# A graph-attention layer whose node tables come from one product of 288 columns, with every edge group gathered from the K/V table

## The reference

```
Q, K, V = x @ Wq + bq, x @ Wk + bk, x @ Wv + bv          # per node
E       = edge_attr @ We + be                            # per edge
score   = exp(clip(sum_d(K[src] * Q[dst] / sqrt(12) * E), -5, 5))   # per edge, head
h       = segment_sum(V[src] * score, dst) / (segment_sum(score, dst) + 1e-6)
out     = layernorm(x + h)
```

## Time and profile before

| what | value |
|---|---|
| timed runs | 1014.6 us median (1014.39 to 1017.43) |
| profiled execution, span | 1301.3 us (this span is all that is recorded of its own time) |
| mean granted TensorE clock in it | 0.729 |
| busy in the span | PE 672.6, PEld 461.0, DVE 653.2, ACT 177.1, POOL 748.1 us |
| DMA | 165.87 MB, 127 GB/s over the span |

### The profile page before, as it was taken

The page is one execution under the profiler, slowest core; times in us unless marked ns, Lnnn a source line. Parts: engine busy times, 40 slices in busy tenths (PEclk is TensorE's granted clock), DMA queues, the critical chain, the costliest instruction groups (busy, mean ns, idle before and its releaser), DMA issues.

```text
span 1301.3 us, 12054 instructions
## 1 busy us (share of the span) xinstructions
PE 672.6 (52%) x3352; PEld 461.0 (35%) x3352; DVE 653.2 (50%) x1307; ACT 177.1 (14%) x337; POOL 748.1 (57%) x788
## 2 busy tenths in 40 slices
PE   3834744755345464455564355545454565445343
PEld 3833422533223343333343233333333333333223
DVE  4311634864346554455554454555455555455446
ACT  1413101111011111011110111011011111111011
POOL 7172465265656665666666565666666666666640
PEclk8756866877677766767778676677767777677777
DMA  7643543544435444544545354544544445445420
GB/s 178 222 145 105 161 126 94 147 125 130 135 100 138 119 132 111 133 132 130 138 120 145 94 153 103 137 134 120 136 131 129 134 128 137 115 136 138 115 70 21
DMA packets 101206, 165.87 MB, mean 127 GB/s; under 512 B 45132, under 2 KB 63853, under 8 KB 101133
## 3 DMA queue, kind: packets, MB, share of 16 engines
q1 hardware_dynamic: 62829, 84.39, 23.4%
q0 software_dynamic: 37152, 75.74, 22.2%
q10 hardware_dynamic: 1152, 4.92, 0.9%
HBM read 152.57 MB, written 12.39 MB: 127 GB/s over the span
## 4 chain that ended last, share of the span: by engine, by line
another core or an unknown queue 40%; issue 22%; DVE 17%; PE 15%; ACT 4%; DMA 1%; DVEq 0%; SPq 0%
DVE qe L830 5%; PE psE L451 4%; DVE logit L919 4%; ACT qe L632 3%; PE psA L521 3%; PE psT L472 3%; DVE qke L910 2%; DVE clipped L925 1%; PE psQ L431 1%; DVE q_parts L809 1%; DVE ob L882 1%; PE psA L482 1%; DVE place L818 1%; DVE msg L937 1%
## 5 line engine op out<-in xcount | busy, mean ns | idle before, releaser
L390 POOL DMA_INDIRECT kv<-kv_table,idx x758 | 724.6, 956 | 514.3 <-issue 218.1
L521 PE MATMUL psA<-place,msg 128*104 128x104 f32 x1536 | 206.4, 301 | 339.7 <-DVE msg L937 253.5
L521 PEld LDWEIGHTS psA<-place,msg 128*104 128x104 f32 x1536 | 193.0, 212 | 369.9 <-DVE msg L937 270.5
L818 DVE TENSOR_TENSOR place<-psI,rel_tile 128x832 f32<-128x832 f32 (+1 forms) x99 | 98.6, 996 | 322.9 <-remote 322.9
L451 PE MATMUL psE<-ea,we 97*96 97x512 f32 x392 | 241.8, 750 | 0.8 <-ACT xt L613 0.8
L632 ACT ACTIVATE qe<-psE 96x1024 f32<-96x1024 f32 (+1 forms) x99 | 99.9, 1009 | 573.4 <-remote 432.5
L830 DVE TENSOR_TENSOR qe<-psQ,qe 96x1024 f32<-96x1024 f32 (+1 forms) x99 | 118.9, 1201 | 60.7 <-ACT qe L632 35.5
L472 PE MATMUL psT<-identity,qe 96*128 96x96 f32 x782 | 109.7, 297 | 74.5 <-DVE qe L830 56.2
L472 PEld LDWEIGHTS psT<-identity,qe 96*128 96x128 f32 x782 | 92.1, 174 | 88.9 <-DVE qe L830 63.8
L910 DVE TENSOR_TENSOR qke<-psT,kv 128x768 f32<-128x768 f32 (+1 forms) x99 | 92.9, 938 | 29.0 <-remote 25.1
L451 PEld LDWEIGHTS psE<-ea,we 97*96 97x96 f32 x392 | 71.5, 206 | 74.5 <-issue 73.5
(11 more groups left out here) (117 smaller groups left out, 405.6 us busy)
## 6 DMA issues: line engine op xcount, KB each, us to landing
ea<-eaT SPq DMA_DIRECT2D x99, 384.0 KB
q_parts<-rel_table SPq DMA_DIRECT2D x99, 252.0 KB
kv<-kv_table,idx POOLq DMA_INDIRECT x758
qwin<-q_table SPq DMA_DIRECT2D x198, 23.6 KB
xb<-xrows SPq DMA_DIRECT2D x24, 144.0 KB
out<-ob SPq DMA_DIRECT2D x24, 144.0 KB
q_table<-q_parts SPq DMA_DIRECT2D x4, 720.0 KB
kv_table<-kv ACTq DMA_DIRECT2D x2, 960.0 KB
```

Of the source, the lines that this page charges most:

```text
L390: pool.indirect_dma_start(kv[:, k, t], None, kv_table, sources).then_inc(kv_in[k], 16)
L521: last = nc.tensor.matmul(sums[0:ML, off:off + PW], msg[:, s, t], place[:, s, t], start=opens, stop=closes)
L818: nc.vector.tensor_tensor(place[:, k % 2, 0:nt], ps_ids.unsqueeze(1).broadcast_to([P, nt, PW]), rel_tile[:, bass.ds(g * T, nt)].unsqueeze( ...
```

## The change

- One product of 288 columns makes the K, V and Q rows of a tile. A pair fills two PSUM banks; three pairs of banks take turns. For each pair ACT makes two copies in place of one: K/V to `kv_stage`, and Q, scaled, to a new buffer `q_full`. PE waits for both copies of the pair three before.
- The ten Q blocks with their own products are gone. `leading` now reads `q_full` and runs between the pairs. `remainder` subtracts in place in `q_full`; five of the ten run before DVE waits for `ranges_all`, and five after the index tables. The middle and last parts follow as before.
- The special path of groups 0 to 2 is gone: raw gathers, transposes, `convert`. All 782 gathers are from `kv_table`, and the first waits for all of it and for the index load, which is now one transfer, issued once `range_up` is counted.
- `CLOSE` goes from 16 to 2: groups 2 to 15 are now also held until the query rows of group *at* - 2 are done.
- SP issues the node chunks with fewer waits, and stores `q_table` in eight chunks in place of six.

```
-CLOSE = 2 * U
+CLOSE = 2
-XG = 3
-Q_CHUNKS = (10, 10, 10, 10, 5, 5)
+EARLY_QUERIES = 5
+        q_full = sb("q_full", [P, NR // P, D], f32)
+        node_banks = [psE, psQ, psT]
@@ block.sync
-                        sp.dma_start(idx[:, 0:XG * T], src[:, 0:XG * T]).then_inc(idx_in, 16)
                         load_nodes(0)
+                        load_nodes(1)
                         sp.wait_ge(xt_in[0], 16)
-                        load_nodes(1)
...
-                        load_nodes(5)
+                        for c in range(5, len(KV_CHUNKS)):
+                            load_nodes(c)
                         sp.wait_ge(range_up, 1)
                         sp.dma_start(range_table..., ranges...).then_inc(range_out, 16)
-                        sp.wait_ge(xt_in[4], 16)
-                        load_nodes(6)
-                        load_nodes(7)
+                        sp.dma_start(idx[:], src).then_inc(idx_in, 16)
                         sp.wait_ge(range_out, 16)
...
-                        sp.dma_start(idx[:, XG * T:], src[:, XG * T:]).then_inc(idx_rest_in, 16)
...
-                            sp.wait_ge(q_up, (tile + size) // QB)
+                            sp.wait_ge(q_up, -(-(tile + size) // QB))
@@ block.gpsimd
                         if first and at == 0:
                             pool.wait_ge(idx_in, 16)
-                        if first and at == XG:
-                            pool.wait_ge(idx_rest_in, 16)
                             pool.wait_ge(kv_out, 16 * len(KV_CHUNKS))
...
-                            if first and at < XG:
-                                pool.indirect_dma_start(xg[:, k, t], None, xrows, sources).then_inc(xg_in[k], 16)
-                            else:
-                                pool.indirect_dma_start(kv[:, k, t], None, kv_table, sources
-                                                        ).then_inc(kv_in[k], 16)
+                            pool.indirect_dma_start(kv[:, k, t], None, kv_table, sources).then_inc(kv_in[k], 16)
@@ block.tensor
-                                if n >= 4:
-                                    pe.wait_ge(kv_up, n - 3)
+                                if n >= 3:
+                                    pe.wait_ge(kv_up, n - 2)
+                                    pe.wait_ge(q_full_up, n - 2)
                                 for j in range(2):
-                                    last = nc.tensor.matmul(kv_banks[n % 4][:, j * 2 * D:(j + 1) * 2 * D],
-                                                            nodes[:, t + j], wn[:, 0:2 * D],
+                                    last = nc.tensor.matmul(node_banks[n % 3][:, j, 0:3 * D], nodes[:, t + j], wn[:],
                                                             start=True, stop=True)
... (the Q products, transposes and convert go)
@@ block.scalar
+                        def leading(n):
+                            act.wait_ge(q_full_up, -(-QB * (n + 1) // 2))
+                            nc.scalar.activation(q_parts[:, n * QB:(n + 1) * QB, 0], q_full[:, n * QB:(n + 1) * QB],
+                                                 ACT.Copy).then_inc(q_hi, 1)
+                        def middle(n):
+                            act.wait_ge(q_r, n + 1)
+                            nc.scalar.activation(q_parts[:, n * QB:(n + 1) * QB, 1], q_full[:, n * QB:(n + 1) * QB],
+                                                 ACT.Copy).then_inc(q_mid, 1)
...
+                            nc.scalar.activation(kv_stage[:, 2 * n:2 * n + 2], node_banks[n % 3][:, :, 0:2 * D],
+                                                 ACT.Copy).then_inc(kv_up, 1)
+                            nc.scalar.activation(q_full[:, 2 * n:2 * n + 2], node_banks[n % 3][:, :, 2 * D:3 * D],
+                                                 ACT.Copy, scale=float(HD) ** -0.5).then_inc(q_full_up, 1)
                             if n in ends:
                                 store_nodes(n)
+                            if 2 * n >= QB * (split + 1):
+                                leading(split)
+                                split += 1
                         store_nodes(NR // P // 2)
+                        for n in range(split, NR // P // QB):
+                            leading(n)
+                        for n in range(NR // P // QB):
+                            middle(n)
@@ block.vector
+                        def remainder(n):
+                            dve.wait_ge(q_hi, n + 1)
+                            nc.vector.tensor_tensor(q_full[:, n * QB:(n + 1) * QB], q_full[:, n * QB:(n + 1) * QB],
+                                                    q_parts[:, n * QB:(n + 1) * QB, 0], ALU.subtract).then_inc(q_r, 1)
+                        for n in range(EARLY_QUERIES):
+                            remainder(n)
                         dve.wait_ge(range_in, 16)
...
-                        remainder(0)
+                        for n in range(EARLY_QUERIES, NR // P // QB):
+                            remainder(n)
                         for n in range(NR // P // QB):
-                            if n + 1 < NR // P // QB:
-                                remainder(n + 1)
                             dve.wait_ge(q_mid, n + 1)
```

More of the change, by code:

```diff
@@ L95, in gnn_program @@
         blank = sb("blank", [P, BW], bf16)
-        xg = sb("xg", [P, XG, T, D], f32)
+        q_full = sb("q_full", [P, NR // P, D], f32)
         identity = sb("identity", [P, P], f32)
@@ L165, in gnn_program @@
         tables_chain, tables_up, rel_out = sem("tables_chain"), sem("tables_up"), sem("rel_out")
-        idx_in, idx_rest_in = sem("idx_in"), sem("idx_rest_in")
-        xg_in = [sem(f"xg_in{i}") for i in range(XG)]
-        turned, turned_up, conv_mm, conv_up = sem("turned"), sem("turned_up"), sem("conv_mm"), sem("conv_up")
+        idx_in = sem("idx_in")
         kv_in = [sem(f"kv_in{i}") for i in range(U)]
@@ L282, in _ @@
                     if first:
-                        for c, (tile, size) in enumerate(chunked(Q_CHUNKS)):
+                        for c, (tile, size) in enumerate(chunked(KV_CHUNKS)):
                             if c == 0:
@@ L290, in _ @@
                                          ).then_inc(q_out, 16)
-                        sp.wait_ge(q_out, 16 * len(Q_CHUNKS))
+                        sp.wait_ge(q_out, 16 * len(KV_CHUNKS))
                     else:
@@ L395, in _ @@
                     for s in range(U):
-                        groups = len(range(s, NG, U)) - (1 if first and s < XG else 0)
+                        groups = len(range(s, NG, U))
                         missing = (T - TAIL_TILES[s]) if s < len(TAIL_TILES) else 0
                         pool.wait_ge(kv_in[s], 16 * (T * groups - missing))
-                    if first:
-                        for s in range(XG):
-                            pool.wait_ge(xg_in[s], 16 * T)
                     nc.gpsimd.dma_reset()
@@ L415, in _ @@
                                 n = (tile + t) // 2
-                                if n >= 4:
-                                    pe.wait_ge(kv_up, n - 3)
+                                if n >= 3:
+                                    pe.wait_ge(kv_up, n - 2)
+                                    pe.wait_ge(q_full_up, n - 2)
                                 for j in range(2):
-                                    last = nc.tensor.matmul(kv_banks[n % 4][:, j * 2 * D:(j + 1) * 2 * D],
-                                                            nodes[:, t + j], wn[:, 0:2 * D],
+                                    last = nc.tensor.matmul(node_banks[n % 3][:, j, 0:3 * D], nodes[:, t + j], wn[:],
                                                             start=True, stop=True)
                                 last.then_inc(kv_mm, 1)
[L423 to L434, removed]
                         pe.wait_ge(we_in, 16)
                         pe.wait_ge(ones_set, 3)
-                        pe.wait_ge(q_r, NR // P // QB)
+                        pe.wait_ge(q_full_up, NR // P // 2)
                     def halves_of(at):
@@ L526, in _ @@
                         pe.wait_ge(ids_up, 2)
[L527 to L549, removed]
                     edge_rows(0, 0, 0)
-                    if first:
-                        for g in range(XG):
-                            convert(g)
                     query_rows(0, 0, 0)
-                    if first:
-                        pe.wait_ge(conv_up, T // 2 * XG)
                     to_rows(0, 0, 0)
@@ L583, in _ @@
+                        split = 0
                         for n in range(NR // P // 2):
                             act.wait_ge(kv_mm, n + 1)
[L585 to L588, removed]
+                            nc.scalar.activation(kv_stage[:, 2 * n:2 * n + 2], node_banks[n % 3][:, :, 0:2 * D],
+                                                 ACT.Copy).then_inc(kv_up, 1)
+                            nc.scalar.activation(q_full[:, 2 * n:2 * n + 2], node_banks[n % 3][:, :, 2 * D:3 * D],
```

(41 more changed lines are left out.)

18 lines of the change are left out of this document (1 added, 17 removed).

## The result

The changed kernel takes 1050.12 us (median of four runs, 1049.7 to 1052.63) against 1015.25 us for the kernel before, a ratio of 1.035 (95% interval 1.0332 to 1.0368): 3.5% slower, as forecast (1050). Two terms of the sum were wrong, with opposite signs, and nearly cancelled: the closeness of the number is in part luck.

What follows compares the result with a forecast made beforehand. The prediction took POOL, issuing gathers almost without a break, to bound the kernel: 1014.6 + 30 (early gathers) + 5 (later table), all else 0, gives 1050 us; range 1041 to 1063.

Steps and rivals of the forecast that it cites:

- What bounds the kernel: POOL issues gathers almost without a break in a timed run, keeping 9.5 us of real waits; table complete at about 42.5.
- The early gathers: 24 gathers on POOL move from before the table to behind it, nothing hides them: +30 us, bounds 22.9 to 38.4.
- The pairs: PE's 288-column products and ACT's copies make the table later: +5 us, bounds -2 to +16.
- The new gate: Group 2's gathers wait for group 0's query rows, forecast at 64 with POOL ready at 67.6: 0, bounds 0 to +9.
- Rival C: Query chain gains nothing, so POOL waits 7 to 9 us before group 2: 1058 us, chance 0.09.
- DVE beside gathers: Gathers starting in DVE's last parts take 1.30 us in place of 0.95: sum 0, bound 3.5 us.
- the port: An allowance of 2 us in the upper end of the range, 1063 us.
- A (consumers set the pace): DVE and PE chain, not POOL, takes some 9 us a group, so faster: 1005 us, chance 0.05.
- B (lead lost anyway): POOL still waits 30 us or more for messages or query rows; change costs 0 to 3: 1016 us, chance 0.05.
- D (lower pace throughout): All PE pairs run at the slow 1.95 us, +16 in place of +5: 1061 us, chance 0.07.

Runs made afterwards that it cites:

- the recording with stops: First profile of the unchanged kernel before, on which the prediction rests: span 1301.3 us, some 287 us of it stops, against a timed median of 1014.6.
- second profile: The kernel before, no edit, profiled once more: span 1014.3 us in an execution of 1016.02 us.
- the kernel without the lead: The kernel before with the raw gathers and conversion of groups 0 to 2 taken out, all 782 gathers from the table: 1043.32 us, 1.0276 of before.

## Why the prediction was right, and where it was not

**What bounds the kernel: right.** The 9.5 us of wait read out of the difference between span and timed median came out as 10.9 (9.7 for the table and 1.2 for messages), and the table came at 43.04 where 42.5 was forecast. Two parts of that reading were off by some 10 us each way: the end of the span, taken with its stops as 29.4, is 17.8; issuing is 722.6 + 229.6 + 23.6 + 7.0 = 982.8 in place of 972.7, because a gather behind a wait has no pause counted, and the recording with stops had more of these.

**The early gathers: right.** +30 forecast, +29.8 measured; the lead removed alone cost 28.0 (0.0276 x 1015), in which 2.7 us of earlier table are already counted as a gain.

**The pairs: the term was mis-sized, +5 against -2.3.** PE in the kernel after:

```profile
8.48 2.28 PE L402 MATMUL psE<-wn,xt 97*128 97x288 f32 x4 [8.48 <-DMA xt<-xT]
10.55 2.12 PE L402 MATMUL psQ<-wn,xt 97*128 97x288 f32 x4
12.47 1.86 PE L402 MATMUL psT<-wn,xt 97*128 97x288 f32 x4
14.16 1.13 PE L402 MATMUL psE<-wn,xt 97*128 97x288 f32 x4
15.13 1.13 PE L402 MATMUL psQ<-wn,xt 97*128 97x288 f32 x4
...
34.53 1.13 PE L402 MATMUL psE<-wn,xt 97*128 97x288 f32 x4
```

And in the kernel before, second profile (x8 are two pairs):

```profile
9.44 2.92 PE L419 MATMUL psE<-wn,xt 97*128 97x192 f32 x8 [9.44 <-DMA xt<-xT]
...
15.06 2.65 PE L419 MATMUL psE<-wn,xt 97*128 97x192 f32 x8
...
18.40 1.07 PE L419 MATMUL psT<-wn,xt 97*128 97x192 f32 x4
19.31 1.98 PE L419 MATMUL psE<-wn,xt 97*128 97x192 f32 x8
...
34.06 0.81 PE L419 MATMUL psE<-wn,xt 97*128 97x192 f32 x4
```

Three things differ from the working. The slow pairs cost 1.7 to 2.1 us, as I had it (1.95), but there are three of them, until 14.16, not 4.2 until 18.1: I tied their end to the clock time at which it came in another kernel. After that a pair of 288 columns takes 0.97 us against 0.89 to 0.96 of 192 (0.92 in the mean from 18.40 to 34.06), and ACT, which I priced at 1.07 by adding single durations, keeps up, because its copies overlap at their edges. So the last pair starts at 34.53 in place of 34.06: +0.5.

And PE alone does not set the end of the table. The last stores of the table, from ACT's queue, in the kernel before, the kernel without the lead (with its last pair) and the kernel after:

```profile
34.92 0.87 ACTq L579 DMA_DIRECT2D kv_table<-kv  x2
```

```profile
32.80 0.81 PE L411 MATMUL psE<-wn,xt 97*128 97x192 f32 x4
33.66 0.84 ACTq L568 DMA_DIRECT2D kv_table<-kv  x2
```

```profile
36.35 0.33 ACTq L520 DMA_DIRECT2D kv_table<-kv  x1
```

In the kernel without the lead the last pair starts 1.7 us before the changed kernel's, and the table is complete only 0.4 us before. From the issue of the last store to the first table gather it is 7.2 us before the change, 5.8 without the lead and 4.0 after it. In stretches of 6 us from 14 to 38 us the DMA engines of these kernels are busy for 0.82 to 1.02 of the time. That the raw gathers' share of this traffic delays the stores fits the 2.7 us, but it was not tested alone: without the lead the first index load goes too, and PE's last pair starts 1.3 us earlier (32.80 against 34.06). In the prediction the earlier table stood as a lower bound (-2), and I chose the other end.

**The new gate: wrong, 0 against +7.0.** The step that failed is "from the end of the last part to the first pick took 10.3 us": in the changed kernel it takes 19.7. The chain in the kernel after (DVE and SP, then PE):

```profile
41.45 5.77 DVE L724 TENSOR_TENSOR q_parts<-q_full,q_parts 128x480 bf16<-128x480 f32 x10
...
62.33 0.96 SPq L229 DMA_DIRECT2D qwin<-q_table  x2
...
66.96 0.49 DVE L734 TENSOR_SCALAR q_parts<-q_parts,query_id 126x1024 bf16<-126x1024 bf16 x1 [19.75 <-DMA q_parts<-rel_table]
...
67.60 1.06 PE L431 MATMUL psQ<-q_parts,qwin 126*96 126x512 bf16 x2 [20.39 <-DVE q_parts L734]
```

SP's wait for the stores of `q_table`, in the kernel after, and then in the first recording of the kernel before with its first windows:

```profile
SPq L223 <- DMA q_table<-q_parts: 11.2, 1, 11.2
```

```profile
SPq L229 <- DMA q_table<-q_parts: 2.1, 1, 2.1
120.90 0.95 SPq L235 DMA_DIRECT2D qwin<-q_table  x2
```

The last parts end at 47.22, earlier than forecast (53), but the pick comes 19.7 us later. This stretch has three pieces. SP issues the last store at 48.1 and waits 11.2 us, so the stores have landed at 59.3, 12.1 us after the last part. Then SP reads where the query windows lie and issues the first of them at 62.33, after 3.0 us. The pick follows 4.6 us later. In the earlier trace rows the same pieces are about 2.5, 3.0 and 4.8 us. So the whole error is in the landing of the stores: there the stops had spread them over 50 us, so that only the last of them was still to land. Packed into 6 us they are a DMA job, with the `ea` loads and the first gathers beside it. DMA share and GB/s (last two columns) of the kernel after:

```profile
48.00:52.00 4.00, 0.00 (x0) 0.00 (x0) 0.00 (x0) 0.27 (x1) 2.98 (x4) 0.50 1.04 423
52.00:56.00 4.00, 0.00 (x0) 0.00 (x0) 0.00 (x0) 0.00 (x0) 2.88 (x4) 0.50 1.02 412
56.00:60.00 4.00, 0.00 (x0) 0.00 (x0) 0.00 (x0) 0.00 (x0) 3.09 (x4) 0.50 0.68 242
60.00:64.00 4.00, 0.00 (x0) 0.00 (x0) 0.00 (x0) 0.00 (x0) 1.60 (x2) 0.50 0.33 82
```

The engines are full while the stores land, and no longer full behind that. The same stretch in the kernel before, second profile:

```profile
59.56 1.41 DVE L799 TENSOR_TENSOR q_parts<-place,q_parts 128x480 bf16<-128x480 f32 x2
73.77 0.55 DVE L809 TENSOR_SCALAR q_parts<-q_parts,query_id 126x1024 bf16<-126x1024 bf16 x1 [12.80 <-DMA q_parts<-rel_table]
```

The kernel's Q rows are ready 14 us earlier than before (47.2 against 61.0), but the first pick comes only 6.8 us earlier (66.96 against 73.77). The Trainium skill (Trainium Kernel Development and Optimization, "Key Constraints") says that transfers from the SP, ACT and POOL queues run on the same 16 engines and interleave, and that issuing from several saves only issue time. The trace agrees as far as it goes: from 48 to 56 us SP's stores and POOL's gathers are under way together, and the 16 engines' share is 1.02 to 1.04.

With the table at 40.7 POOL is ready for group 2 at 61.9 (67.6 forecast), 7 us before the product of group 0's query rows ends. Rival C had this as its mechanism, "the gate bites", at 7 us; the cause it named, an unshortened Q chain, is not the one, and that its number fits is chance (74.5 - 67.6 there).

The two errors are not independent. Behind the gate POOL goes on when the query rows are there, whenever the table was complete: at 68.93, where the forecast has 67.6. So the gate takes back what the earlier table gave, and the sum comes out right. That the query rows, forecast at 64 by a wrong step, came so close to 67.6 is luck.

**DVE beside gathers: right that it is small.** In the changed kernel the first four gathers start beside the remainders and the ten last parts, which run without a break from 38.60 to 47.22. (The prediction had the remainders end before the first gather; they end at 41.53, the first gather starts at 40.71.) The four gathers take 1.21, 1.26, 1.40 and 1.40 us against 0.95, so 1.5 us in all; in the kernel before two such gathers take 1.27 and 1.37. The mean of all 782 is 953 ns, the same as before. The range's upper end counts 2 us for "the port": no run shows a port, only these 1.5 us.

**The other rivals.** A (consumers set the pace): DVE waits 333.8 us for gathers in the kernel after, so no. B (lead lost anyway): the kernel without the lead is 28 us slower, so no. D (lower pace throughout): three pairs of 25 are slow, so no.

What stays open is why PE's first pairs run at half pace in a stretch whose granted clock the windows give as 1.00, and what made the stops of the one recording.

## What to carry to other kernels

When one engine issues without a break, write the sum on that engine alone: what is moved across its start counts in full, and everything else counts only where it ends one of its waits. Compare the span of a profile with the timed runs before reading any duration between engines from it; single instructions kept their length in the recording with stops (956 and 953 ns), but intervals that contain transfers did not. A gate is priced by when the transfers ahead of it have all landed, at the rate of full DMA engines where they are packed, and by the steps that follow the landing (7.7 us here); an interval read where the same transfers were spread out does not give it.

## What the runs showed of the hardware

A gather of 128 rows by index costs POOL about 0.95 us and a pause of 0.30 whether the rows have 384 or 768 bytes (nearly every row of either kind; means 959 and 956 ns in the first recording). It takes 1.21 to 1.40 us when it starts beside one of DVE's subtractions with two SBUF operands (0.65 us each). Behind the slow first pairs, at a granted clock of 1.00, a pair of tiles with fp32 products of 288 columns costs 0.97 us against 0.89 to 0.96 for 192, as the spacing of their records: half again as many columns for 1 to 9% more time. Eight stores of 3.7 MB issued within 6 us, with 1.6 MB of loads ahead and gathers beside them, had landed 12 us after the last part of Q was ready.
